# Expert blocks in pairs: a shared transpose and two row tiles for the last 48 inner columns

## The reference

```python
logits = x @ gate_weight.T                      # x: 1024 x 256
topk_w, topk_idx = jax.lax.top_k(softmax(logits), 6)
topk_w = topk_w / (topk_w.sum(-1, keepdims=True) + 1e-20)
for e in range(28):
    h = jax.nn.silu(x @ w_gate[e]) * (x @ w_up[e])      # 1024 x 176
    y += cw[:, e, None] * (h @ w_down[e])               # cw: topk_w scattered, 0 elsewhere
```

## Time and profile before

| | us |
|---|---|
| median of 3 runs | 864.53 |
| lowest, highest run | 862.65, 871.02 |
| profiled execution, its time | 870.67 |
| profiled execution, its span | 868.7 |
| PE busy in the span | 743.6 (86%) |
| DVE, ACT, POOL busy | 488.3, 329.5, 311.7 |
| mean granted TensorE clock | 0.908 |

### The profile page before, as it was taken

How to read it: one execution, slowest core, us unless ns; L and a number is a source line. 1 busy time by engine, 2 the same in 40 slices (tenths; PEclk the granted TensorE clock), 3 DMA queues, 4 the chain that set the end, 5 groups by cost and what they waited for, 6 DMA issues and landing times. The chain is left out here.

```text
span 868.7 us, 14703 instructions
## 1 busy us (share of the span) xinstructions
PE 743.6 (86%) x4795; PEld 543.4 (63%) x4802; DVE 488.3 (56%) x1397; ACT 329.5 (38%) x1012; POOL 311.7 (36%) x300
## 2 busy tenths in 40 slices
PE   4899998989878898789899899997237999999990
PEld 2756677777635477677775686665125777777770
DVE  2445658888664845455664466556132555555563
ACT  2245535555510141254544646675002222222220
POOL 2022443444410402122230130505652666666661
PEclk9699999999899999967887799999567999999995
DMA  9999993000232006965711003911844666666657
GB/s 319 301 350 350 350 361 151 2 1 2 97 146 97 1 0 129 126 90 39 86 25 25 1 1 113 404 49 59 341 170 103 107 109 112 112 106 110 113 62 212
DMA packets 91863, 115.78 MB, mean 133 GB/s; under 512 B 18380, under 2 KB 84109, under 8 KB 90766
## 3 DMA queue, kind: packets, MB, share of 16 engines
q1 hardware_dynamic: 77964, 97.94, 39.4%
q0 software_dynamic: 13104, 16.52, 12.2%
q10 hardware_dynamic: 722, 0.37, 0.2%
HBM read 58.18 MB, written 56.63 MB: 132 GB/s over the span
## 5 line engine op out<-in xcount | busy, mean ns | idle before, releaser
L709 PE MATMUL PS<-W_all,fgu 128*128 x600 | 179.8, 423 | 0.4 <-issue 0.2
L709 PE MATMUL PS<-R 32*128 32x128 f32 (+10 forms) x1196 | 154.0, 379 | 18.9 <-DMA R<-scrq 3.7
L709 PEld LDWEIGHTS PS<-R 32*128 32x128 f32 (+4 forms) x1196 | 96.6, 192 | 60.0 <-issue 35.3
L709 PEld LDWEIGHTS PS<-W_all,fgu 128*128 128x128 f32 x600 | 103.3, 192 | 22.0 <-issue 2.6
L2042 ACT ACTIVATE R<-PS 128x512 f32<-128x512 f32 (+5 forms) x163 | 79.3, 540 | 88.7 <-PE PS L717 51.1
L717 PE MATMUL PS<-ident,R 128*128 128x128 f32 x606 | 93.4, 300 | 10.1 <-POOL R L2461 2.4
L717 PEld LDWEIGHTS PS<-ident,R 128*128 128x128 f32 x606 | 74.4, 155 | 35.2 <-issue 19.6
L2487 POOL DMA_INDIRECT y<-fwd,xh x45 | 69.9, 1554 | 54.4 <-DVE fwd L2009 52.7
L2398 POOL TENSOR_TENSOR R<-R 128x512 f32<-128x512 f32 x44 | 44.8, 1040 | 87.7 <-DVE R L1520 87.7
L1988 DVE TENSOR_TENSOR fwd<-PS,fwd 128x176 f32<-128x176 f32 x75 | 25.6, 341 | 84.7 <-ACT fwd L2351 84.7
L2388 POOL TENSOR_TENSOR rs<-rs,mh 128x1 f32<-128x1 f32 x48 | 26.9, 562 | 123.9 <-DVE rs L1421 123.6
(11 more groups left out here) (293 smaller groups left out, 1461.7 us busy)
## 6 DMA issues: line engine op xcount, KB each, us to landing
xg<-zrow SPq DMA_DIRECT2D x28, 1088.0 KB, 12.2
xh<-xg SPq DMA_DIRECT2D x45, 136.0 KB, 2.5
W_all<-in_wgu SPq DMA_DIRECT2D x1, 5760.0 KB, 21.1
W_all<-in_wgu SPq DMA_DIRECT2D x1, 5280.0 KB, 27.7
R<-in_wqkv SPq DMA_DIRECT2D x1, 4096.0 KB, 17.9
xT<-xg SPq DMA_DIRECT2D x30, 136.0 KB, 2.5
y<-zrow SPq DMA_DIRECT2D x3, 1152.0 KB, 11.7
scrq<-bqkv SPq DMA_DIRECT2D x12, 256.0 KB, 4.8
```

What stands on the lines that cost most here:

```text
L709: return e.matmul(out, l, r, start=start, stop=stop, skip_group_check=True)
```

## The change

Blocks are taken in pairs q = (2q, 2q+1); block 74 stays alone.

- `W_all` loses the last 48 rows of w_down (WE = 960). Instead SP loads these rows, 48 KB, per block: a pair's two go into one tile `w2` (three of them), at partitions 0 to 47 and 64 to 111 (`ld2`). `mp` writes their offsets to `blocks`, with one more DVE instruction.
- `et` takes a pair: four transposes into one bank, one ACT copy. It waits for both x tiles. `xbT` has two pair tiles instead of three block tiles.
- `eu` stays per block. DVE puts the products of a pair side by side into `HM` (368 columns: the first block's 176, 16 zeros, the second block's last 48 at 192, its first 128 at 240); for a pair's second block it needs two instructions. ACT's silu now waits for `sg` to be read.
- `eh` takes a pair: three transposes (first 128 of the one, both blocks' last 48 together, first 128 of the other), one DVE copy of 384 columns.
- `ed` takes a pair: the first down matmul of both blocks, then a wait for `w2`, then both blocks' last matmul over 48 rows each, at partitions 0 to 47 and 64 to 111, into banks 5 and 6.
- The order is now, per pair: `ldx` of two blocks, `ld2` of pair q+2, `ed` q-1, `eh` q, `et` q+2, `eu` of blocks 2q+2 and 2q+3. `eh` has one bank instead of two.
- Accumulators: the last six blocks alternate between 0 and 1 (`ACC`), so that number 2 is complete after block 68. At the end number 2 is loaded first, then 0, then 1, each in four quarters with a semaphore each, and DVE adds quarter by quarter. The landing tiles `yb` no longer lie on `W_all`.

```diff
-WE = 1216
+WE = 960
+ACC = [j % NY for j in range(NB - 6)] + [0, 1, 0, 1, 0, 1]
+NTH = [ACC[:j].count(ACC[j]) for j in range(NB)]
...
+        for q in range(2):
+            add("et", q, banks=[q])
+        for j in range(2):
+            add("eu", j, banks=[2 + j])
+        for q in range(NPAIR + 1):
+            for j in (2 * q + AHEAD, 2 * q + AHEAD + 1):
+                if j < NB:
+                    add("ldx", j)
+            if q + 2 < NPAIR:
+                add("ld2", q + 2)
+            if q:
+                add("ed", q - 1, banks=[5, 6][:len(blocks_of(q - 1))])
+            if q < NPAIR:
+                add("eh", q, banks=[4])
+            if q + 2 < NPAIR:
+                add("et", q + 2, banks=[q % 2])
+            for j in (2 * q + 2, 2 * q + 3):
+                if j < NB:
+                    add("eu", j, banks=[2 + j % 2])
...
+            def ld2(q):
+                if q >= 3:
+                    for u in fills("ed", q - 3):
+                        e.wait_ge(u.full, u.f + 1)
+                for j in blocks_of(q):
+                    r = number(256 + j, (NE - 1) * 48)
+                    rows = slice(64 * (j % 2), 64 * (j % 2) + 48)
+                    e.dma_start(w2[q % 3][rows, :], D["wd2"][bass.ds(r, 48), :]).then_inc(sem(f"w2_{q % 3}"), 16)
...
             def out():
-                for i in range(NY):
-                    e.wait_ge(sem(f"y{i}"), 16 * (NB // NY))
-                    e.dma_start(yb[i], D[f"y{i}"][0:1024, :].rearrange("(t p) n -> p t n", p=128)).then_inc(sem(f"yb{i}"), 16)
+                for i in (2, 0, 1):
+                    e.wait_ge(sem(f"y{i}"), 16 * ACC.count(i))
+                    for q in range(4):
+                        src = D[f"y{i}"][256 * q:256 * q + 256, :].rearrange("(t p) n -> p t n", p=128)
+                        e.dma_start(yb[i][:, 2 * q:2 * q + 2, :], src).then_inc(sem(f"yb{i}_{q}"), 16)
...
+            def eh(q):
+                u, h = fill("eh", q), HM[q % 2]
+                for j in blocks_of(q):
+                    w = fill("eu", j)
+                    e.wait_ge(w.free, w.k + 1)
...
+                for i, at in enumerate((0, 128, 240)[:len(blocks_of(q)) + 1]):
+                    a = tr(u.t[:, i * 128:i * 128 + 128], h[:, at:at + 128])
+                a.then_inc(u.full, 1)
+
+            def ed(q):
+                us, w = fills("ed", q), fill("eh", q)
                 e.wait_ge(w.free, w.k + 1)
...
+                for u, j in zip(us, blocks_of(q)):
+                    room(u)
+                    mm(u.t[:, 0:256], hT_[q % 2][:, 2 * (j % 2), :], w_(j, 704, 256), True, False)
+                e.wait_ge(sem(f"w2_{q % 3}"), 32 * (q // 3) + 16 * len(us))
+                for u, j in zip(us, blocks_of(q)):
+                    rows = slice(64 * (j % 2), 64 * (j % 2) + 48)
+                    mm(u.t[:, 0:256], hT_[q % 2][rows, 1, :], w2[q % 3][rows, :], False, True).then_inc(u.full, 1)
...
+                if j % 2 == 0:
+                    e.tensor_tensor(h[:, 0:176], u.t[:, 176:352], g, ALU.mult).then_inc(u.free, 1)
+                else:
+                    e.tensor_tensor(h[:, 240:368], u.t[:, 176:304], g[:, 0:128], ALU.mult)
+                    e.tensor_tensor(h[:, 192:240], u.t[:, 304:352], g[:, 128:176], ALU.mult).then_inc(u.free, 1)
```

More of the change, by code:

```diff
@@ L275, in experts @@
             add("ldx", j)
[L276 to L289, removed]
+        add("ld2", 0)
+        add("ld2", 1)
+        for q in range(2):
[17 more added lines that the diff above has]
+                    add("eu", j, banks=[2 + j % 2])
         add("out")
@@ L1972, in mp @@
                 own.mark(e.tensor_scalar(blocks[0:1, 0:75], u7.t[0:1, 0:75], float(NE - 1), float(WE), ALU.min, ALU.mult))
+                own.mark(e.tensor_scalar(blocks[0:1, 256:331], u7.t[0:1, 0:75], float(NE - 1), 48.0, ALU.min, ALU.mult))
                 own.mark(e.tensor_copy(ejb, u7.t[:, 256:331]))
@@ L1990, in eh @@
-            def eh(j):
-                u = fill("eh", j)
-                e.wait_ge(u.full, u.f + 1)
[L1993 to L2009, removed]
+                if j % 2 == 0:
+                    e.tensor_tensor(h[:, 0:176], u.t[:, 176:352], g, ALU.mult).then_inc(u.free, 1)
+                else:
+                    e.tensor_tensor(h[:, 240:368], u.t[:, 176:304], g[:, 0:128], ALU.mult)
+                    e.tensor_tensor(h[:, 192:240], u.t[:, 304:352], g[:, 128:176], ALU.mult).then_inc(u.free, 1)
@@ new lines, in eh, with ed @@
+            def eh(q):
+                u, n = fill("eh", q), len(blocks_of(q)) + 1
+                e.wait_ge(u.full, u.f + 1)
+                if q >= 2:
+                    for w in fills("ed", q - 2):
+                        e.wait_ge(w.full, w.f + 1)
+                e.tensor_copy(hT_[q % 2][:, 0:n, :], u.t[:, 0:128 * n].rearrange("p (c n) -> p c n", n=128)).then_inc(u.free, 1)
+            def ed(q):
+                for j, u in zip(blocks_of(q), fills("ed", q)):
+                    r, w = xb[j % NX], wk6[j % 2]
+                    e.wait_ge(sem(f"xb{j % NX}"), 16 * (j // NX + 1))
+                    own.mark(e.scalar_tensor_tensor(out=w[:, 0:6], in0=r[:, 262:268], scalar=ejb[:, j:j + 1], in1=r[:, 256:262],
+                                                    op0=ALU.is_equal, op1=ALU.mult))
+                    again()
+                    own.mark(e.tensor_reduce(w[:, 6:7], w[:, 0:6], X, ALU.add))
+                    e.wait_ge(u.full, u.f + 1)
+                    if j >= 3:
+                        e.wait_ge(sem(f"y{ACC[j - 3]}"), 16 * (NTH[j - 3] + 1))
+                    again()
+                    e.tensor_scalar(ys[j % 3], u.t[:, 0:256], w[:, 6:7], None, ALU.mult).then_inc(u.free, 1)
@@ L2350, in eu @@
                 e.wait_ge(u.full, u.f + 1)
+                if j >= 2:
+                    w = fill("eu", j - 2)
+                    e.wait_ge(w.free, w.k + 1)
                 e.activation(sg[j % 2], u.t[:, 0:176], ACT.Silu).then_inc(sem("sg"), 1)
```

111 lines of the change are left out of this document (55 added, 56 removed).

## The result

| | before | after |
|---|---|---|
| median, us (20 runs each, side by side) | 869.16 | 862.88 |
| ratio, 95% interval | | 0.9933 (0.9903 to 0.9962) |
| profiled execution, its time / span | 870.67 / 868.7 | 867.14 / 865.3 |
| from SP's first load of an expert row tile to the end | 214.5 | 208.5 |

The change takes 0.67% off, 6 us. The forecast, 857.3 of 864.53, is a ratio of 0.9916 and lies in the interval; so does its sign. What the prediction held likeliest in words, no difference that one can tell, did not come: the interval is 0.3% to either side, not the 1% that I took a measurement of this kernel to resolve.

What follows compares the result with a forecast made beforehand. PE was taken to bound the expert stage. Steady pairs -7.0, start +1.5, drain and end -1.7 sum to -7.2 us, taking 864.53 to 857.3 us (-0.8%), range 848 to 870.

Steps and rivals of the forecast that it cites:

- What bounds the stage: Expert stage: PE is busy for all 180.00 us of the window at clock 1.00, so only its stream counts.
- The steady pair, 4.98 to 4.78: PE's stream per pair of blocks: 0.20 us less, about 35 times, 7.0 us in all.
- the change of shape is free: Rival, last down products: leaving the array's 128-row shape costs nothing, 0.54 us less per pair, 845.4 us; chance 0.08.
- the twins run in turn: Rival, pair's two 48-row last down matmuls: the second waits for the first, +0.23 us per pair, 872.4 us; chance 0.07.
- No bubble: Steady pairs: PE never waits; joint transposes need a 1.1 us round trip, covered by 1.59 us of PE work.
- the rival of a late round trip: Joint transposes wait on ACT and DVE; at 2.0 us 14.4 us are lost, 871.7 us; chance 0.15.
- Start, +1.5: Start of the expert stage: later x tiles and an open round trip cost 1.5 us, between 0.5 and 2.5.
- Drain and end, -1.7: Last blocks and final accumulator reads: counted from the same PE position, the end comes 1.7 us earlier.
- 2 to 4 us late: Drain: the last scatter comes this late, as the last six scatters alternate on two accumulators.
- 0.6 to 2.6 us earlier: End, counted from the same PE position: net gain from the early accumulator read and quarterwise adds; 1.7 taken.
- PE stalls about 1.5: Drain: the last lone block waits for the copy behind two scalings, so PE idles about 1.5 us.
- No difference as the likeliest outcome: Whole kernel: time within 1% of before, chance 0.54, against 0.33 for faster and 0.13 for slower.

Runs made afterwards that it cites:

- Doing without the twins: Changed kernel with each last down product over all 128 rows, one after the other, instead of two simultaneous 48-row matmuls: 0.9973 of the kernel before.
- half the excursions: Down products of four blocks grouped, with 16 row tiles, 5 `w2` and 5 `ys`, against the kernel before: ratios 0.9892 and 0.9881.
- by fours: Down products of four blocks grouped instead of two, accumulators j mod 3, pair 1's transposes later, tile counts unchanged: 1.0037 of the kernel before.
- accumulators in turn: Changed kernel with accumulators j mod 3 to the end, read in order 0, 1, 2: ratios 0.9885 and 0.9935 to the kernel before.

## Why the prediction was right or wrong

- **What bounds the stage: right.** PE is busy but for the ends, at clock 1.00, in both kernels, and each hundredth of a microsecond in its stream counted 35 times.
- **The steady pair, 4.98 to 4.78: right** in each term, with the twins in twos and 0.09 to 0.10 at each change of shape. Doing without the twins (4.86) and with half the excursions (9.21 for four blocks) priced the two halves of it apart. The rivals in which the change of shape is free or the twins run in turn fall with that: the one needs 4.44 and the other 5.21.
- **No bubble: right.** The second product is done 0.63 us ahead of the joint transposes; the rival of a late round trip, from 1.59 us, does not occur. That cover is thin elsewhere: by fours, landings that pairs never felt cost 1 to 2 us in every second period.
- **Start, +1.5: right in size** (+1.3). The first product came 0.93 late, 0.22 of it was done early, and PE stood still for 0.89 in the open round trip; the sum of these is 1.6, so some 0.3 came back from the clock, where I had 0.5. That the clock also takes back a part of what one gains there I did not see.
- **Drain and end, -1.7: the step of the sum that failed.** It measured -0.3, 1.4 us short; the whole sum, -7.2 against -6.0, is off by little else. (By the other two profiles of the changed kernel it is -1.0 and -0.2, all against one profile of the kernel before.) What lies behind the last scatter was right: "2 to 4 us late" and "0.6 to 2.6 us earlier" make 4.6 us gained there, and it was 4.5 (18.9 us from last scatter to end before, 14.4 after). The lateness was too small: the last scatter came 1.5 us earlier where PE had led by 5.7, so 4.2 late, and -1.7 holds 2.9. The prediction had "PE stalls about 1.5" and PE stalled 3.82. I had priced the landing beside a 1 MB read at "5 to 6", and it was 6.2; but I let it delay only the scatters of the alternation and not what else waits for a landing, the scaling's tile of `ys`, with the lone block's copy queued on DVE behind it and PE behind that. The run with the read held back has the 1.56 and its last scatter 3.4 us earlier than before the change. It does not end earlier, because the read then stands behind the last scatter: that run shows the cause of the stall, and not that the -1.7 was to be had without it.
- **No difference as the likeliest outcome, by a bound of one per cent: the step of the call that failed.** With 20 runs a side the interval is 0.3%, and 0.67% less is told from nothing. The sum itself said 0.8% less; the chance of 0.54 on no difference rested on a resolution that no run had shown, and said too little of what I had worked out.

## What to carry to other kernels

Small row tiles pay by the excursion, not by the matmul: price entering and leaving (here 0.34 us for both and what they uncover) against what one visit saves, and gather visits before giving up on them. When a transfer is started early beside a pipeline that still drains, list every wait for a landing there, the free-buffer waits too, and what is queued behind each on its engine. And where an engine's clock is still low, work brought forward is worth less than the time by which it is brought forward (here 0.3 of 0.7 us).

## What was not expected of the hardware

After PE's idle 3.82 us the last matmuls ran at the low clock. Windows of the changed kernel, the stall's and the one behind it:
```profile
840.46:846.81 6.35, 2.13 (x11) 1.19 (x11) 2.61 (x10) 0.32 (x1) 2.54 (x3) 0.88 0.78 197
846.81:849.30 2.49, 2.36 (x4) 0.99 (x4) 0.25 (x2) 0.00 (x0) 2.19 (x2) 0.50 0.30 35
```
and of accumulators in turn, where PE's idle time is 1.57:
```profile
852.00:854.10 2.10, 0.69 (x3) 0.36 (x3) 1.39 (x6) 0.00 (x0) 1.55 (x1) 1.00 0.54 62
854.20:855.20 1.00, 0.97 (x2) 0.26 (x2) 0.00 (x0) 0.00 (x0) 1.00 (x1) 0.50 0.88 89
```
```profile
853.41 0.69 PE L740 MATMUL PS<-W_all,fgu 128*128 x2 [1.57 <-DVE fgu L2043]
854.04 1.14 PE L740 MATMUL PS<-xT,fgu 48*128 48x256 f32 x2
```
The first two down halves take 1.14 in the one (846.81 to 847.95) and 0.63 in the other (853.41 to 854.04). But it is not the length of the stall that makes the difference: the clock fell 188.5 us from SP's first load in the one (a mean of 0.88 over the 6.35 us puts it at 845.3) and 188.6 us from it in the other (between 854.10 and 854.20). In the other these two halves were done by then; in the one they were still to come. Work that slips behind the fall of the clock pays twice, here some 0.5 us beyond the stall itself. And the landing of a scatter, 3.8 us in the median before and 4.1 after, is no constant: the one issued 0.9 us after a 1 MB read began took 6.2.
